# The opening and the ending of a fused transformer layer follow the steady instruction order instead of orders written out by hand

## What is computed

```python
x = rotate(x, theta, phi)                             # pairs of features turned by per-batch angles
x = layernorm(x + gelu(x @ Wi[e]) @ Wo[e]) * g + b    # e: one of 8 experts, 256 -> 1024 -> 256
# c == 0, 1: two-matmul branch; c == 2: three-matmul branch (256 -> 512 -> 256 -> 256)
x = layernorm(x + branch[c](x)) * gamma + beta
x = layernorm(x) * (1 + scale(t)) + shift(t)
q, k, v = x @ Wq, x @ Wk, x @ Wv                      # 16 heads of 16
p = softmax(q @ k.T / 4 + bias[b, head], masked)      # bias: 32 x 16 x 256 x 256
x = x + (p @ v) @ Wo
x = x + gelu2((layernorm(x) * g2 + beta2) @ W1) @ W2  # 256 -> 1024 -> 256
```

## Time and profile before

| what | value |
|---|---|
| median of 3 runs | 2135.9 us (2134.21 to 2136.43) |
| the profiled execution | 2134.21 us, span in the profile 2132.4 us |
| PE busy | 1943.4 us, 91% of the span |
| VectorE, ScalarE, GpSimd busy | 1605.9, 1358.5, 294.0 us |
| mean granted TensorE clock | 0.98 of full speed |
| DMA | 356 MB, 167 GB/s on average |
| chain that ended last | PE 66%, VectorE 20%, no wait seen 7%, ScalarE 4% |

### The profile page before, as it was taken

How to read it: one execution, slowest core, us unless ns; L and a number is a source line. 1 busy time by engine, 2 the same in 40 slices (tenths; PEclk the granted TensorE clock), 3 DMA queues, 4 the chain that set the end, 5 groups by cost and what they waited for, 6 DMA issues and landing times.

```text
span 2132.4 us, 43394 instructions
## 1 busy us (share of the span) xinstructions
PE 1943.4 (91%) x14133; PEld 1681.0 (79%) x14354; DVE 1605.9 (75%) x5373; ACT 1358.5 (64%) x2177; POOL 294.0 (14%) x393
## 2 busy tenths in 40 slices
PE   5789999999999999999999999999999999999786
PEld 4678888888888788888888887888888888778665
DVE  4467877787887788887777887777888877776764
ACT  3266676677667676667667666666676676666443
POOL 1101111011111011111011111101111110111100
PEclk9789999999999999999999999999999999999899
DMA  6654645565554565654565655556565545653450
GB/s 211 193 176 152 184 151 147 184 196 180 184 168 135 161 191 186 193 167 155 146 191 176 190 171 164 156 177 195 181 190 183 168 146 166 205 161 108 128 151 14
DMA packets 222312, 356.13 MB, mean 167 GB/s; under 512 B 29523, under 2 KB 120147, under 8 KB 222068
## 3 DMA queue, kind: packets, MB, share of 16 engines
q1 hardware_dynamic: 222068, 352.99, 53.4%
HBM read 294.12 MB, written 58.79 MB: 165 GB/s over the span
## 4 chain that ended last, share of the span: by engine, by line
PE 66%; DVE 20%; issue 7%; ACT 4%; DMA 2%; SPq 1%; POOL 0%; ACTq 0%; DVEq 0%; POOLq 0%
PE pD L470 43%; PE pX L685 11%; PE pS L470 9%; DVE bias_ring L1171 8%; DVE bias_ring L968 6%; PE pC L470 2%; PE pC L707 1%; DVE x_nat L965 1%; DMA branch_row<-in_branch_rows 1%; ACT L775 1%; DVE crossed L965 1%; ACT gelu_out L775 1%; ACT probs L775 1%; SPq L294 1%; ACT hid L775 0%
## 5 line engine op out<-in xcount | busy, mean ns | idle before, releaser
L1171 DVE CUSTOM_DVE_ANT_0 bias_ring<-pS,bias_ring 128x256 f32<-128x256 f32 x1024 | 389.3, 417 | 215.9 <-PE pS L470 212.1
L775 ACT ACTIVATE probs<-pX 128x512 f32<-128x512 f32 x512 | 304.5, 595 | 257.4 <-PE pX L685 255.3
L775 ACT ACT_TABLE_LOAD x340 | 436.2, 1283 | 23.1 <-PE pD L470 16.3
L685 PE MATMUL pX<-ident,bias_ring 128*128 128x128 f32 x2048 | 326.9, 283 | 110.6 <-DVE bias_ring L968 92.7
L685 PEld LDWEIGHTS pX<-ident,bias_ring 128*128 128x128 f32 x2048 | 228.7, 142 | 210.7 <-DVE bias_ring L968 198.8
L968 DVE TENSOR_SCALAR bias_ring<-bias_ring,row_max 128x256 f32<-128x256 f32 x1024 | 337.0, 371 | 18.3
L470 PE MATMUL pS<-k_stack,q_stack 96*128 96x256 f32 x1024 | 305.3, 380 | 0.6 <-DMA k_stack<-k_spill 0.3
L470 PE MATMUL pD<-x,raw 128*128 128x256 f32 x1024 | 250.3, 388 | 4.5 <-ACT gelu_out L775 3.7
L470 PE MATMUL pD<-raw,gelu_out 128*128 128x256 f32 x1024 | 239.6, 381 | 3.3 <-DVE y_nat L965 3.3
L470 PEld LDWEIGHTS pS<-k_stack,q_stack 96*128 96x128 f32 x1024 | 198.6, 194 | 20.2
L470 PEld LDWEIGHTS pD<-x,raw 128*128 128x128 f32 x1024 | 190.4, 194 | 30.5 <-issue 7.3
(11 more groups left out here) (148 smaller groups left out, 3690.2 us busy)
## 6 DMA issues: line engine op xcount, KB each, us to landing
bias_ring<-in_fside SPq DMA_DIRECT2D x512, 256.0 KB, 3.5
raw<-in_experts SPq DMA_DIRECT2D x128, 512.0 KB, 4.3
q_spill<-hid SPq DMA_DIRECT2D x96, 256.0 KB, 3.4
k_spill<-hid SPq DMA_DIRECT2D x96, 256.0 KB, 3.4
q_stack<-q_spill SPq DMA_DIRECT2D x128, 192.0 KB, 3.6
k_stack<-k_spill SPq DMA_DIRECT2D x64, 384.0 KB, 4.9
norm<-in_expert_rows SPq DMA_DIRECT2D x32, 384.0 KB, 4.0
x_nat<-in_x SPq DMA_DIRECT2D x32, 256.0 KB, 3.2
```

The source lines that it names most:

```text
L685: last = e.transpose(pX[:, k, t * P:(t + 1) * P], bias_ring[:, u % NBIAS, t, k * P:(k + 1) * P], ident[:, :])
L775: return e.activation(o, i, func, bias=bias, scale=scale)
L1171: e.tensor_tensor_reduce(bias_ring[:, n, t, :], pS[:, t, :], bias_ring[:, n, t, :], 1.0, -3.4e38, ALU.add, ALU.max, row_max[:, n, t:t + 1] ...
```

## The change

The two strings `FIRST` and `LAST` are removed. The loop takes `ORDER` 36 times. At the start of each engine's list a number of `f`, `h` and `r` steps is left out (`SKIP`), so that the streams begin one after the other; at the end a stream that has run out does nothing.

```diff
-FIRST = {
-    "PE": (
-        "gggggggggffffgfgfggfggfgggfhhhhhhhhhfhhffhghhghhhgghhgfhhghhhfhhhgfhhghhghhfhhhhfhhhhhhhhhhfrhhf"
...
-LAST = {
-    "PE": (
-        "hhhhhhhhfhhfrhhfhhhrhhhfghhrhhghhhhhhfrhhrghhghghfrhggrfhhhrhhghhrhhfhhhhghhfhhrrhhfhhfhhrrhhrhh"
...
-OUTSIDE = 7
+
+SKIP = {"PE": (9, 101, 37), "ACT": (13, 56, 55), "DVE": (12, 53, 47), "POOL": (4, 0, 6), "SP": (10, 42, 4)}
...
+            skip = dict(zip("fhr", SKIP[engine]))
             next(extra, None)
-            for letter in FIRST[engine] + ORDER[engine] * (NB - OUTSIDE) + LAST[engine]:
-                next(streams[letter], None)
+            for _ in range(NB + 4):
+                for letter in ORDER[engine]:
+                    if skip.get(letter):
+                        skip[letter] -= 1
+                    else:
+                        next(streams[letter], None)
```

## The result

The changed kernel takes 2160.0 us (median of 4 runs, 2157.8 to 2169.1), the kernel before 2135.1 us in the same session: ratio 1.0117, 95% interval 1.0101 to 1.0134. The prediction was 2142.0, in a range of 2130 to 2156. "Slower" was right; the size was not, 25 us in place of 6, and the time lies above the range.

The account below looks back on a forecast made before the run. PE was taken to bound a steady pass's first half, with VectorE about as full in the second. Opening +11.3 and ending -5 gave +6.3 us on the profiled 2134.2: 2140.5, or 2142.2 against the median; range 2130 to 2156.

Parts of the forecast that it names:

- The opening up to the first exponential: From 60.6 us to head 0: wide steps now run ahead of q, k, v; first exponential at 125.5 us, 28 later.
- The chain after v: Between v_aug and the first scores: a three-matmul branch of batch 1, rotation, gT.2 and gi0.2 take 18.8 us at full clock.
- Heads 7 to 23: Opening: a steady pass of 61.1 us less four absent steps (5.8, all in its first half), 55.4 with rounding.
- PE bounds the first half: Steady pass, first nine heads, 29.1 us: TensorE sets the time, while VectorE has only 20.05 us of work.
- Heads 0 to 7: Opening, just after the first exponential: VectorE's and PE's work counted, PE 26 us with its gaps; 27 us.
- Pass 32: Ending: loses its nine wide steps, 61.1 - 1.7 - 3.1 = 56.3, plus 2.5 for the low clock: 58.8 us.
- pass 33: Ending: nine heads at 2.63 us, one at 4.0, then 23.3 us: 51 us, against 53.5 before.
- The last heads: Ending, the last eight heads up to head 511: 22.4 us, against 22.5 before.
- before has a wait of 5.20 us for the branch row: Ending, pass 30: why the steady 61.1 us is not quicker than the 60.1 of the kernel before.
- The ends meet: Rival, no change: each order reaches heads 39 and 511 with the same work done; +4.5 and -5, 2135 us; chance 0.24.
- faster, by the ending: Rival: steady order ends VectorE and PE waiting in turn in passes 30 to 33; 2127.5 us, chance 0.17.
- The low clock spreads: Rival: short PE groups from 79 to 100 us and in pass 32 run at low clock; +19 and +2, 2157 us; chance 0.13.

Follow-up runs that it names:

- the ending alone: Kernel with the opening written out by hand as before and the changed kernel's passes 30 to 35 at the end: 2140.5 us, ratio 1.0025 to the kernel before.

## Why the prediction was wrong

- *The opening up to the first exponential* was right in its result (+30.2 for +28) and in the gaps of q, k and v. The chain after v was right by luck (a wait for the write of k in place of a three-matmul branch).
- *Heads 7 to 23, "the steady pass of 61.1 without rn1, rh3, rn2 and rn3 (4 x 1.44 = 5.8, all in its first half): 55.4"* is the step that failed. It took 65.7 us. 4.3 of the difference is the three-matmul branch, which lies here and not between heads 23 and 39 (61.0 us, where 65.4 was predicted). The rest is that the four steps, priced at 5.8 us, gave 0.4: their first half took 33.2 us with TensorE busy for 27.2, a full one with the same branch 33.6 with 31.3. "PE bounds the first half" had been read from a busy share of 93%; 38 us less work in 23 such halves gave 0.1 us, while putting the division later gave 12. Heads 0 to 7 took 28.4, not 27. Together the stretch was 7.3 us too short.
- *Pass 32, "61.1 - 1.7 - 3.1", and pass 33, "51"* failed in the same way: 60.8 and 55.3, where 58.8 and 51 stood. Nine wide steps less gave back next to nothing, since, by the rows shown above, a head without filler costs its own chain, with the division in it and in part at the lower clock. The last heads took 24.2, not 22.4. This is 8.1 of the 8.6 us by which the ending missed up to head 511. With the ending alone the two passes took 59.1 and 53.0, less of the time at the lower level, so part of these misses is the clock's. Behind head 511 another 1.7 us are missing (+0.8 for -0.9), with the clock at 0.76 where it was 0.86 before.
- *"before has a wait of 5.20 us for the branch row"* was given as the reason why a steady pass 30 is not quicker. The sum took no credit for it, and 61.2 us came where 61.1 stood. The row is on the path, as its earlier load shows, but mostly in the middle, where the change leaves it; of the 11 us heads 39 to 439 gave 11.0 (1560.2 for 1571.2), and heads 439 to 511 nothing that can be told (262.1 for 262.9).
- *The rivals.* "The ends meet" and "faster, by the ending" took the same step for granted and fell with it. "The low clock spreads" gave 2157 and came nearest, but in the opening its mechanism is not what cost. By the clock column about 36 us were spent at the lower level from 60.6 us to head 39 before (0.18 x 36.8 + 0.07 x 164.6, over 0.5) and 43 after, and TensorE's busy time grew by 1.2 us of the 20.7. The gaps cost, not the speed between them. The warning of the Trainium skill ("TensorE: Matmul & The Clock Gate", HAM oscillation) on short matmul groups held (0.70 over 67 us, where it was 0.82 over 36.8); its price was small in the opening and part of the 4.4 us in the ending.
- *The range.* It was said to take in the low clock's case, but that case stood at 2157 and the range ended at 2156.

## What to carry to other kernels

A busy share of 93% does not mean that removing that engine's work shortens a pass: where engines run through fixed lists in step, price a removed step only after following the chain without it. A stretch of the same trace that already lacks the step, or a run that leaves its work out, tells it by halves of a pass. In an opening, count the idle time of the busiest engine up to a point behind which nothing changed; moving the first result earlier is worth nothing unless that idle time shrinks. Waits say little by their sum: 477 us less of one was worth 11 us, 34 us less of another 15, and only moving the work that they stood in told it.

## What was not expected of the hardware

The same list of the last 72 heads took between 262.2 and 267.3 us in different profiled runs, with the granted clock of its passes 32, 33 and the last heads at 0.91, 0.90 and 1.00 in the one and 0.89, 0.88 and 0.93 in the other. Most of the difference, 3.8 us, is longer busy time of TensorE.
